# A graph network kernel: the eight-head attention sums stay in PSUM over all seven chunks, and its edge lists are packed during the gated layer

## The reference, cut to what matters

```python
h = maximum(layernorm(x), 0) @ W_map + b_map
hh = (h @ W1).reshape(n, 8, 8)                      # 8 heads, 8 channels each
logits = leaky_relu(a_src[src] + a_dst[dst], 0.2)   # one per edge and head
m = segment_max(logits, dst);  e = exp(logits - m[dst])
denom = segment_sum(e, dst)
out = segment_sum(hh[src] * e[:, :, None] / denom[dst][:, :, None], dst)
```

## Time and profile before

| | |
|---|---|
| runs, median (lowest to highest) | 3260.48 us (3255.64 to 3260.98) |
| profiled execution, its span | 3254.36 us, 3252.2 us |
| gated layer's stream | 1051 to 2297 us |
| MLP stage with the edge tables | 2297 to 2376 us |
| edge phase, first gather to last join | 2378 to 2945 us |
| PE, DVE, ACT, POOL busy (share of span) | 2812.0 (86%), 1828.0 (56%), 1375.2 (42%), 924.1 us (28%) |

### The profile page before, as it was taken

One profiled execution on the slowest core, in us unless ns is written; L12 is line 12 of the kernel. 1 busy time (PEld: TensorE's weight loads), 2 busy tenths in 40 slices (PEclk: granted clock), 3 DMA queues, 4 the chain that ended last, 5 costly groups with the idle time before them and its releaser, 6 DMA issues. The chain is left out here.

```text
span 3252.2 us, 44556 instructions
## 1 busy us (share of the span) xinstructions
PE 2812.0 (86%) x15308; PEld 2176.7 (67%) x15308; DVE 1828.0 (56%) x4352; ACT 1375.2 (42%) x2647; POOL 924.1 (28%) x734
## 2 busy tenths in 40 slices
PE   5777886999996999999999999999866666676997
PEld 3445774677774878778787787887445555564775
DVE  8998657999977541121121113111556666666994
ACT  4574234999996221111111112111353433333896
POOL 6110070000001643223232231331057777740000
PEclk9999997999998999999999999999957777776999
DMA  5333442111002432112122121320243222103200
GB/s 164 137 116 137 192 180 91 42 42 61 27 1 80 187 133 91 66 61 101 61 89 78 61 96 41 117 96 1 68 102 75 63 48 48 39 17 131 82 36 21
DMA packets 90231, 266.52 MB, mean 82 GB/s; under 512 B 22048, under 2 KB 70007, under 8 KB 80311
## 3 DMA queue, kind: packets, MB, share of 16 engines
q1 hardware_dynamic: 74783, 238.32, 19.9%
q0 software_dynamic: 15232, 25.35, 3.7%
HBM read 232.33 MB, written 31.29 MB: 81 GB/s over the span
## 5 line engine op out<-in xcount | busy, mean ns | idle before, releaser
L3109 PE MATMUL psum<-gate_stream,parts 128*128 128x384 f32 (+1 forms) x3600 | 667.7, 344 | 8.6 <-ACT x L3149 4.4
L3109 PEld LDWEIGHTS psum<-gate_stream,parts 128*128 128x128 f32 x3600 | 630.4, 188 | 25.6 <-issue 6.1
L3214 POOL CAST gate_stream<-gate_adj 128x1920 fp32r<-128x1920 f16 (+1 forms) x200 | 371.7, 1866 | 834.9 <-PE psum L3109 824.1
L2467 PE MATMUL psum<-gat_h,gat_pair 128*128 128x129 f32 (+1 forms) x3750 | 542.5, 290 | 17.0 <-DVE gat_pair L2271 15.3
L2467 PEld LDWEIGHTS psum<-gat_h,gat_pair 128*128 128x128 f32 (+1 forms) x3750 | 458.3, 191 | 128.2 <-DVE gat_pair L2271 67.1
L3247 DVE SCALAR_TENSOR_TENSOR gate_work<-psum,bhh,gate_work 128x384 f32<-128x384 f32 (+1 forms) x80 | 50.1, 626 | 779.1 <-PE psum L3056 763.2
L1691 POOL DMA_INDIRECT edge_rows<-edge_table,src_idx x388 | 390.8, 1007 | 166.6 <-issue 121.4
L2271 DVE SCALAR_TENSOR_TENSOR gat_pair<-gat_above,gat_adj 128x512 f32<-128x512 f32 (+3 forms) x525 | 325.2, 619 | 73.7 <-PE psum L2467 35.8
L2371 ACT ACTIVATE psum<-gat_ad_rows,gat_as 128x512 f32<-128x512 f32 (+3 forms) x525 | 334.9, 638 | 16.8
L2380 ACT ACTIVATE gat_above<-psum,gat_as 128x512 f32<-128x512 f32 (+3 forms) x525 | 324.5, 618 | 40.8 <-PE psum L2455 38.4
L2226 DVE SCALAR_TENSOR_TENSOR gat_acc<-gat_adj,gat_q,gat_acc 128x512 f32<-128x512 f16 (+3 forms) x497 | 327.8, 676 | 0.0
(11 more groups left out here) (502 smaller groups left out, 3997.0 us busy)
## 6 DMA issues: line engine op xcount, KB each, us to landing
gate_adj<-adj SPq DMA_DIRECT2D x35, 2400.0 KB, 8.2
gat_adj<-adj SPq DMA_DIRECT2D x8, 3200.0 KB, 10.9
gcn_adj<-adj SPq DMA_DIRECT2D x10, 2400.0 KB, 8.2
adj<-count_stage SPq DMA_DIRECT2D x196, 100.0 KB, 1.7
edge_place_wide<-row_scratch SPq DMA_DIRECT2D x110, 128.0 KB, 3.2
gate_adj<-adj SPq DMA_DIRECT2D x5, 2800.0 KB, 9.1
gcn_adj<-adj SPq DMA_DIRECT2D x2, 3200.0 KB, 10.4
edge_rows<-edge_table,src_idx POOLq DMA_INDIRECT x388
```

The lines of the kernel that those rows point to most:

```text
L2467: mm = e.matmul(ps[0:p, b, a:a + D + 1], pair[:, g % 2, i * P:i * P + p], h1[:, hi, h, :], start=hi == 0 and i % 3 == 0, stop=hi == NT - 1 ...
L3109: mm = e.matmul(ps[:, f, 0:hi - lo], parts[:, t, m, f, :], stream[:, (NGG * i + t // GG) % GR, 0:windows(i), t % GG * W:(t % GG + 1) * W], ...
L3214: e.tensor_copy(stream[:, n % GR, 0:windows(i), :], cols[:, i % 2, 0:windows(i), g * GW:(g + 1) * GW]).then_inc(widened, 1)
```

## The change

Two parts. **The sums.** PSUM is cleared once, before chunk 0, and all chunks add to the same banks; the accumulator is joined once, after chunk 6. For this a chunk's maxima start from the last one of the chunk before (`carry[:, 0:1]` in place of -1e30). Only a node that goes on over a chunk's border may then have been summed with a lower maximum. Its row is picked out of the copied sums by a matmul (`node_of`, `hold`), and a matmul of one row adds what is missing (`fix_held`, at step 4 of the chunk). **The tables.** `EdgePacks` takes the loading, packing and storing of the edge lists out of the MLP stage into the gated layer; the count moves from q = 2 to q = 0; `vector_places` moves ahead of the first `stat`, and its second half is a function of its own behind that `stat`.

```diff
 # gated_steps: SP's order, DVE's order (POOL also gets one iota ahead of its first cast)
+                    if i == 4:
+                        packs.sync_loads(e)      # six DMAs, after blank
+                    if i == 9:
+                        packs.sync_stores(e)     # one DMA, 832 KB, after made
...
+                    if i == 1:
+                        packs.vector_blanks(e)   # two memsets, behind gates(0)
+                    if i == 6:
+                        packs.vector_packs(e)    # L294 to L304, behind gates(5)
 # load_dense
+            e.wait_ge(packs.stored, 16)
             e.dma_start(x1t[:, 0:ND], away[1, :, 0:ND]).then_inc(ahead, 16)
 # MLP stage, SP
-                edges.sync_loads(e)
+                e.dma_start(flat_x, away[0, :, :]).then_inc(x_in, 16)
...
-                e.dma_start(flat_x, away[0, :, :]).then_inc(x_in, 16)
-                edges.sync_tiles(e)
 # MLP stage, PE
-                    if q == 2:
+                    if q == 0:
                         edges.tensor_count(e)
 # MLP stage, DVE
                 edges.vector_rows(e)             # now without L289, L291 and L294 to L304
                 weights(e)
+                edges.vector_places(e)           # L337 to L339
                 e.wait_ge(x_in, 16)
...
                     if q == 0:
+                        edges.vector_marks(e)    # L341 to L354
                         weights_turned(e)
...
-                    if q == 2:
-                        edges.vector_places(e)
 # edge_chunks, DVE, per chunk
+                    if c:
+                        e.wait_ge(carries_up, c)
+                        e.tensor_copy(carry[:, 0:1], carry[:, KP:KP + 1]).then_inc(passed, 1)
+                        e.wait_ge(passed, 3 * (c - 1) + 1)
                     e.wait_ge(ends_up, c + 1)
...
+                    if c:
+                        ease_held(c)             # two operations on 1 x 8
                     e.wait_ge(weights, c + 1)
                     for at in (slice(0, half), slice(half, n)):
                         e.tensor_tensor(... channels(weight[:, at]), ALU.mult).then_inc(marks, 1)
+                        if c and at.start == 0:
+                            fix_held(c)          # three operations on 1 x 64, 1 x 8, 1 x 9
                     ahead = of_chunk[c + 1]
                     if ahead:
-                        find([(ahead[0], 0, HEAD)])
-                    if c:
-                        join_most(c - 1)
-                    if ahead:
-                        find([(ahead[0], HEAD, NT)])
-                    if c:
-                        join_sums(c - 1)
+                        find([(ahead[0], 0, NT)])
...
-                join_most(end)
-                join_sums(end)
+                join_most()
+                join_sums()
 # edge_chunks, ACT: take(c - 1) waits for held, no longer for joined; per chunk
+                    if c:
+                        e.wait_ge(node_up, c)
+                        e.copy(node_col[:], node_up_to).then_inc(node_in, 1)
                     ...exponentials L1924, L1925...
                     if c:
-                        ease_off(c - 1)
+                        e.wait_ge(passed, 3 * c)
+                        e.activation(ease[:], ease[:], ACT.Exp).then_inc(eases, 1)
 # edge_chunks, PE
+                def node_of(c):
+                    e.wait_ge(hots, 2 * share * c + 2)
+                    ...
+                    e.transpose(node_up_to, hot[0:1, 0, :], self.ident[0:1, 0:1]).then_inc(node_up, 1)
+                def hold(c):
+                    e.load(part_regs, self.part_r[0:1, c:c + 1])
+                    ...
+                    e.wait_ge(node_in, c)
+                    e.wait_ge(taken, c)
+                    e.matmul(held_row, node_col[:], flat_part[:, bass.ds(at, SUMS)], start=True, stop=True).then_inc(held, 1)
...
+                        if c and s == HELD_AT:
+                            e.wait_ge(fixed, c)
+                            e.matmul(flat[:, bass.ds(to_first, SUMS)], hot[0:1, 0, :], fix[:], ...).then_inc(fixes, 1)
...
                     line_up(c)
+                    if c:
+                        node_of(c)
                     ends_of(c)
                     carries_of(c)
+                    if c:
+                        hold(c)
                     peaks_of(c)
-                    clear(c)
+                    if c == 0:
+                        clear()
                     sums(c)
```

More of the change, by code:

```diff
@@ L231, in __init__, with gpsimd @@
         self.first, self.first_f = sb("first", [ER, ETR], I32), sb("first_f", [ER, ETR])
         self.tile_no, self.some = sb("tile_no", [ER, ETR]), sb("some", [ER, ETR])
+        self.blank, self.loaded, self.made, self.stored, self.numbered = (
+            nc.alloc_semaphore("packs_" + n) for n in ("blank", "loaded", "made", "stored", "numbered"))
+    def gpsimd(self, e):
+        e.iota(self.tile_no[:], [[1, ETR]], base=0, channel_multiplier=ETR, allow_small_or_imprecise_dtypes=True).then_inc(
+            self.numbered, 1)
@@ new lines, in sync_stores, with vector_blanks, vector_packs @@
+    def sync_stores(self, e):
+        e.wait_ge(self.made, 1)
+        e.dma_start(self.k.edge_scratch.rearrange("(p g) w -> p (g w)", g=ETR),
+                    self.pack.rearrange("p g c q -> p (g c q)")).then_inc(self.stored, 16)
+    def vector_blanks(self, e):
+        e.memset(self.di, NP)
+        e.memset(self.si, 0).then_inc(self.blank, 1)
+    def vector_packs(self, e):
+        made = self.made
+        row = lambda t, at: t[:, at:at + EPR].rearrange("p (g q) -> p g q", g=ETR)
+        e.wait_ge(self.loaded, 6 * 16)
+        e.tensor_copy(self.pack[:, :, 0, :], row(self.si, 0))
+        e.tensor_copy(self.pack[:, :, 1, :], row(self.di, 1))
+        e.tensor_tensor(self.pack[:, :, 2, :], row(self.di, 1), row(self.di, 0), ALU.not_equal)
+        e.tensor_tensor(self.pack[:, :, 3, :], row(self.di, 1), row(self.di, 2), ALU.not_equal).then_inc(made, 1)
+        e.wait_ge(self.numbered, 1)
+        e.tensor_scalar(self.some[:], self.tile_no[:], 1.0, None, ALU.min)
+        e.tensor_scalar(self.first[:], self.di[:, 1:EPR + 1:P], 7, None, ALU.arith_shift_right).then_inc(made, 1)
+        e.wait_ge(made, 2)
+        e.tensor_tensor(self.first_f[:], self.first[:], self.tile_no[:], ALU.add).then_inc(made, 1)
+        e.wait_ge(made, 3)
+        e.tensor_tensor(self.first_f[:], self.first_f[:], self.some[:], ALU.mult).then_inc(made, 1)
@@ L287, in vector_rows @@
         k, ps, made = self.k, self.ps, self.made
-        row = lambda t, at: t[:, at:at + EPR].rearrange("p (g q) -> p g q", g=ETR)
-        e.memset(self.di[:], NP)
         e.memset(self.tile_i[:], 0)
-        e.memset(self.si[:], 0).then_inc(made, 1)
         e.memset(self.one[:], 1.0)
[L293 to L297, removed]
-        e.wait_ge(self.drawn, 1)
[L299 to L305, removed]
+        e.wait_ge(self.drawn, 1)
+        e.wait_ge(self.packs.made, 4)
         for g in range(ETR):
-            inst = e.tensor_scalar(self.reached[:, g, :], self.step_row[0:ER, :], self.first_f[:, g:g + 1], None, ALU.is_ge)
+            inst = e.tensor_scalar(self.reached[:, g, :], self.step_row[0:ER, :], self.packs.first_f[:, g:g + 1], None, ALU.is_ge)
         inst.then_inc(made, 1)
@@ L1636, in edge_chunks @@
         size, first_step = CHUNKS, CHUNK_AT
+        assert all(at == KP * c for c, at in enumerate(first_step))
         by_pool = [size[c] - DRAWN[c] for c in range(end + 1)]
@@ L2077, in _ @@
                         e.wait_ge(drawn, of_chunk[c + 1][-1] + 1)
-                for r in out_regs + tab_regs:
+                for r in out_regs + tab_regs + part_regs + first_regs:
                     e.free_register(r)
@@ L2082, in edge_chunks @@
             second, peaks_up, falls, weights, filled, marks, hots, summed, taken, present, eased, joined,
-            copied, spread, packed, ones, pulled, drawn, split, begun] + fetched + place_in + src_in)
+            copied, spread, packed, ones, pulled, drawn, split, passed, node_up, node_in, held, eases, fixed, fixes, begun] + fetched + place_in + src_in)
         st.close()
```

180 lines of the change are left out of this document (109 added, 71 removed).

## The result

The changed kernel took 3237.52 us (median of 4 runs, 3233.57 to 3242.09) against 3258.12 us (median of 4) for the kernel before: ratio 0.9944, 95% interval [0.9932, 0.9956]. Measured again later on another chip it was 0.9955 [0.9942, 0.9969], 3240.76 against 3254.30 us. The profiled execution took 3242.09 us, its span is 3240.3 us; before it was 3252.2, so 11.9 us are to be found in the traces.

What follows compares the result with a forecast made beforehand. POOL's gathers were taken to pace the edge phase, DVE the MLP stage's end and PE the gated layer; -15.9 + 0.8 - 7.5 + 4.9 = -17.7 us gave 3236.7 or 3242.8, forecast 3240 us between them, range 3228 to 3253.

Steps and rivals of the forecast that it cites:

- the likeliest case: Whole kernel: the forecast itself, 3240 us, with its own range of 3232 to 3250 us and a chance of 68%.
- Term 1: Edge phase: without a join in each chunk, POOL's gathers are no longer slowed beside it, -15.9 us.
- the count of the triples: Edge phase: three long gathers beside each of five joins, 2.56 + 4 x 3.33 = 15.9 us.
- The 12% rival: Edge phase: the joins don't slow POOL, so the sum is -1.8 us, 3256 us; chance 12%.
- The side beside it: Edge phase: DVE and PE's own time per chunk falls from 70.4 to 64.5 us, so POOL stays the pace.
- The stall and the half clock behind it: PE in the sums: its 3.53 us stall falls to 0.5, and 5.8 us at half clock go, worth 2.9.
- The clearing matmuls: PE ahead of each chunk's sums: five matmuls removed from its 4.80 us of idle time, worth nothing.
- Term 2: Edge phase, the held row: hidden by DVE's wait in chunks 1 to 5, +0.8 us in chunk 6.
- the slower rival: Edge phase: the held row's chain across PE, ACT and DVE becomes the pace, 3276 us; chance 3%.
- Term 3: MLP stage: earlier count and fetches, split table work, two PE waits gone and one new of about 2 us, -7.5 us.
- half of the tail's half-clock time saved: MLP stage's tail, 18.41 us busy at a mean clock of 0.59: half of its half-clock time goes.
- Term 4: Gated layer: packing behind gates(5) lengthens PE's wait from 2.87 to 5.4 us, 2.5 plus 2.4 for the clock, +4.9 us.

Runs made afterwards that it cites:

- tables_only: The kernel before with only the tables' part (`EdgePacks`, new order of the MLP stage), its joins left in place: 3256.06 us, ratio 1.0000.
- sums_only: The kernel before with only the new `edge_chunks`, its table work left in the MLP stage, plus one small copy: 3242.62 us, ratio 0.9954.
- two_reads: The changed kernel plus three `tensor_tensor` operations with both inputs in SBUF per chunk (1 to 6), where the joins stood: 3257.12 us, ratio 1.0004.
- best: The changed kernel with packing behind gates(9), busy matmuls in the MLP tail and chunk 6, 30 ahead of chunk 6's sums: 3225.37 us, ratio 0.9913.
- packs_late: The changed kernel with the packing behind gates(9) instead of gates(5) and the store at i = 13: ratio 1.0008 to the kernel before, slow chip.
- all_three: The changed kernel with packing behind gates(9), busy matmuls in the MLP tail and chunk 6, 16 ahead of its sums: ratio 0.9999, slow chip.
- busy_c6: The changed kernel with 16 busy matmuls ahead of chunk 6's sums and one behind each step of their first half: ratio 1.0020, slow chip.

## Why the prediction was right, and where a term was off

The time lies 2.5 us under the forecast of 3240 us and inside the likeliest case's own range. That it lies so close is in part luck. The four terms were forecast at -17.7 us and measured at -11.6 in the profiled pair; the medians differ by 20.6 us here, but by 13.5 in the second measurement and by 13.5 for the sums alone. Two terms were too large, both to the same side, and the first pair of medians fell 7 us further apart than the second. The main mechanism and its size are right for reasons that the runs show.

**Term 1 (-15.9) measured -13.7.** The mechanism is shown: taking the joins away shortens the gathers' stretch from 512.2 and 512.6 us (before, `tables_only`) to between 498.2 and 498.8 us (`sums_only` and two traces of the changed kernel), putting three operations of their kind back restores it (512.1 us in `two_reads`), and three of equal length with one input don't (497.5 us). POOL's busy time fell by 15.1 us, 0.8 short of the count of the triples. Another 1.3 us went to POOL's issue gaps (121.4 to 122.7 us), nearly all to one gap of 3.28 us that was 2.01. The 12% rival, that the joins don't slow POOL, is out.

The side beside it, DVE and PE, was forecast to fall from 70.4 to 64.5 us a chunk and fell to 72.69 - 5.63 = 67.1. The stall and the half clock behind it went as said, but the sums start 0.8 us later in the chunk, and the clock rises 6.0 us into them in place of 3.9. The clearing matmuls, which the forecast held to be worth nothing, used to fill part of PE's wait ahead of the sums: its idle time there is 7.14 us in place of 4.80. Whether that is why the clock rises later, no run tests. DVE's wait for gathers did not grow to about 6 us; it is 2.5 to 5.6 us. That cost nothing, since POOL is still last.

**Term 2 (+0.8) measured +0.8 to +1.1.** In chunk 6 the sums start 19.60 us behind the first logits, before 18.81. In the other chunks DVE's wait hides it, and PE has no wait at step 4 in any chunk. Of the slower rival (3276) nothing shows.

**Term 3 (-7.5) measured -3.8, the term that was mis-sized.** Its early steps came as walked: fetches from 2311.6 (the whole stage lies 4.85 us later), the places read at 2323.15, the waits of 2.23 and 2.76 us gone, one new wait of 2.10 us at the turn-back of the fourth piece. The step that failed is "half of the tail's half-clock time saved": none of it was. The clock fell at the 2.10 us wait and stayed down to the end. With PE kept busy through that wait (mean clock 0.88 from 2350 to 2371 us in `best`) the stage takes 73.35 to 73.86 us, 7.1 to 7.6 under the kernel before, which is the forecast's number. So the missing 3.7 us are the clock's. (The same stage took 82.22 us in `sums_only`, where it differs from before by one small copy: single executions of a stage scatter by about 1 us.)

**Term 4 (+4.9) measured +4.85**, and the wait 5.30 us for 5.4. Moving the packing gave 2.3 us back in `packs_late`, where the clock fell all the same, and about 4 in `all_three` and `best`, where it held, so the split into 2.5 and 2.4 was about right as well. The forecast's worry that POOL's casts slow the packing came true only where it was moved to: behind gates(9) it takes 5.7 us in place of 2.5, and nobody waits for it.

## What to carry to other kernels

Before counting what an operation costs its own engine, ask what stands beside it: here 8 us of DVE work per chunk were free for DVE, and cost POOL three stalled gathers; operations with one SBUF input in the same place cost nothing. When work is moved under a wait, look whether the engine that waits was already waiting there, since the stalls add up and may take the clock with them. And where nothing covers a stretch at half clock, try to fill the wait ahead of it with busy matmuls: two such fillings and one moved block gave 15.4 us here, about as much as the change itself.

## What the runs showed of the hardware that was not expected

- PE can be busy without a gap and stay at half clock. The sums of chunk 6 filled 6.00 of 6.00 us of both PE and the weight load at 0.50 from 2905 to 2917 us; the clock rose at 2917.5, only after 128x256 bf16 matmuls stood between the steps (from 2914.0 on). The kernel before shows the same (18 us of sums at 0.50). With such matmuls between the steps from the first one on (`busy_c6`) it rose 8.5 us into the sums.
- How long PE waited did not alone decide its clock. A wait of 2.87 to 2.90 us at the same place of the same stream was followed by full clock in three of the five traces without the early packing (the kernel before, `all_three`, `best`: 0.63 us for four transposes). In `packs_late` the transposes behind it ran at half clock (1.09 us), and in `sums_only` they were still quick (0.63), but from 1171 to 1173 us the clock was 0.50. Behind 5.30 us it was half in all seven traces with the early packing, and behind 2.10 us in the MLP stage too. In the trace before, a wait of 2.76 us was already followed by half clock and one of 2.87 us by full.
- The contention goes both ways. The packing's second cast, 0.42 us behind gates(5), took 2.02 us behind gates(9), and an operation on 104 x 4 took 1.78 us for 0.16. Each ended within 0.3 us of a cast of POOL's beside it (1313.06 to 1315.09 and 1316.53 to 1318.33). Timeline of DVE, `packs_late`:

```profile
1313.03 0.42 DVE L265 CAST x1t<-x1t 104x512 f32<-104x512 int32 x1
1313.36 2.02 DVE L266 CAST x1t<-x1t 104x512 f32<-104x512 int32 x1
...
1316.57 1.78 DVE L271 TENSOR_SCALAR packs_first<-x1t 104x4 int32<-104x4 int32 x1
```

- One of the three chips used for the experiments ran the kernel before 12% slower (3654.69 us). In the four traces taken there, all of the changed kernel's kind, SP's queue moves nothing for over 130 us while POOL's gathers run, though loads are issued; in the changed kernel's trace on another chip both go side by side. A gain on the engine that sets the pace on one chip may be worth nothing on another.
